# A recurrent cell computed by halves of its columns, with the last slot sums added straight out of PSUM

## The reference

```python
x = x + 0.5 * ffn(layernorm(x))
x = x + attn(layernorm(x))
x = x + 0.5 * ffn(layernorm(x))
```

```python
alpha = top-8 softmax of gelu(x @ w1.T + b1) @ w2.T      # T x 64
gi = (alpha.T @ x) / (alpha.sum(0) + 1e-8)               # 64 x 512 per sequence
gx = gi @ gru_wih.T + gru_bih ; gh = hs @ gru_whh.T + gru_bhh
r = sigmoid(xr + hr) ; z = sigmoid(xz + hz) ; n = tanh(xn + r * hn)
h_new = (1 - z) * n + z * hs
out = alpha @ (h_new @ wv.T + bv) @ wo.T + bo
```

## Time and profile before

| what | value |
|---|---|
| median of three runs | 3039.88 us (3039.07 to 3040.82) |
| the profiled execution | 3037.27 us, span 3035.4 us |
| PE busy | 2731.7 us (90%) |
| DVE busy | 1970.5 us (65%) |
| ACT busy | 1035.0 us (34%) |
| POOL busy | 1330.8 us (44%) |
| granted TensorE clock, mean | 0.964 of full speed |
| chain that ended last | PE 58%, DVE 29%, issue 8%, DMA 3% |

### The profile page before, as it was taken

How to read it: one execution, slowest core, us unless ns; L and a number is a source line. 1 busy time by engine, 2 the same in 40 slices (tenths; PEclk the granted TensorE clock), 3 DMA queues, 4 the chain that set the end, 5 groups by cost and what they waited for, 6 DMA issues and landing times.

```text
span 3035.4 us, 116733 instructions
## 1 busy us (share of the span) xinstructions
PE 2731.7 (90%) x51036; PEld 1942.8 (64%) x51036; DVE 1970.5 (65%) x5236; ACT 1035.0 (34%) x1891; POOL 1330.8 (44%) x1768
## 2 busy tenths in 40 slices
PE   7999789899899999999998999999999999989867
PEld 6787456666666666666666666666666666666643
DVE  6776456666666666666666666666766676666625
ACT  5776222333333333333233233333333332323220
POOL 2221444545444445444454445445555444445410
PEclk9999889999999999999999999999999999999978
DMA  7351112212122222212222222212122222212177
GB/s 228 96 162 52 41 47 67 56 32 59 53 60 60 60 60 60 58 55 52 60 60 56 56 60 60 56 44 51 53 60 60 60 60 59 63 46 56 42 257 290
DMA packets 365962, 224.75 MB, mean 74 GB/s; under 512 B 277584, under 2 KB 294032, under 8 KB 365456
## 3 DMA queue, kind: packets, MB, share of 16 engines
q1 hardware_dynamic: 356240, 200.51, 24.1%
q10 hardware_dynamic: 9216, 16.78, 1.5%
HBM read 125.49 MB, written 74.97 MB: 66 GB/s over the span
## 4 chain that ended last, share of the span: by engine, by line
PE 58%; DVE 29%; issue 8%; DMA 3%; POOL 1%; ACT 1%; SPq 1%; DVEq 0%; POOLq 0%; ACTq 0%
PE psum L875 14%; DVE blk L3133 10%; DVE blk L3131 10%; PE psum L1028 5%; PE psum L970 4%; PE psum L1050 4%; PE psum L1069 4%; PE psum L994 4%; PE psum L1037 4%; PE psum L779 2%; PE psum L951 2%; PE psum L1007 2%; PE psum L1090 2%; PE psum L930 2%; PE psum L716 1%
## 5 line engine op out<-in xcount | busy, mean ns | idle before, releaser
L875 PE MATMUL psum<-w_all,xnT 128*128 128x512 f32 (+2 forms) x2048 | 746.8, 501 | 21.3 <-DVE xc L3032 17.4
L2473 POOL TENSOR_TENSOR sm<-sm,half 128x1 f32<-128x1 f32 (+1 forms) x384 | 535.0, 1393 | 122.6 <-ACT sm L2048 106.6
L875 PEld LDWEIGHTS psum<-w_all,xnT 128*128 128x128 f32 x2048 | 363.9, 191 | 190.3 <-issue 145.0
L3131 DVE TENSOR_TENSOR blk<-blk 128x30 f32<-128x30 f32 (+14 forms) x960 | 398.8, 415 | 77.5 <-issue 50.7
L3133 DVE TENSOR_TENSOR blk<-blk 128x30 f32<-128x30 f32 (+14 forms) x960 | 427.2, 445 | 33.1
L930 PEld LDWEIGHTS psum<-xnT,w_all 128*128 128x128 f32 x2048 | 270.5, 202 | 75.6 <-issue 71.5
L930 PE MATMUL psum<-xnT,w_all 128*128 128x128 f32 x2048 | 295.6, 291 | 4.0 <-issue 4.0
L1050 PE MATMUL psum<-qg,st 32*32 32x64 f32 x8192 | 189.4, 228 | 87.8 <-DVE st L3149 53.8
L1069 PE MATMUL psum<-w_out,gate 128*128 128x512 f32 x512 | 253.0, 613 | 4.6 <-issue 2.5
L1050 PEld LDWEIGHTS psum<-qg,st 32*32 32x32 f32 x8192 | 140.6, 111 | 175.6 <-DVE st L3149 90.4
L3149 DVE STREAM_TRANSPOSE st<-psum 128x128 f32<-128x128 f32 x256 | 81.0, 316 | 201.2 <-PE psum L1050 198.2
(11 more groups left out here) (276 smaller groups left out, 4645.8 us busy)
## 6 DMA issues: line engine op xcount, KB each, us to landing
blk<-n_scratch SPq DMA_DIRECT2D x64, 512.0 KB, 4.4
xin<-in_L_attn_x_dram SPq DMA_DIRECT2D x96, 256.0 KB, 4.8
xh<-xc SPq DMA_DIRECT2D x64, 256.0 KB, 2.3
n_scratch<-nn SPq DMA_DIRECT2D x64, 256.0 KB, 3.4
e_scratch<-blk SPq DMA_DIRECT2D x32, 512.0 KB, 2.6
E<-e_scratch SPq DMA_DIRECT2D x64, 256.0 KB, 3.9
x_scratch<-xh SPq DMA_DIRECT2D x62, 256.0 KB, 3.7
rxn<-in_L_attn_x_dram SPq DMA_DIRECT2D x32, 256.0 KB, 2.9
```

The lines of the kernel that those rows point to most:

```text
L875: last = mm(dst, xnT[b][:, k * P:(k + 1) * P], w_all[:, k * WK + at:k * WK + at + n], start=(k == 0), stop=(k == KC - 1))
L2473: return g.tensor_tensor(dst, a, half[:, 0:n], ALU.pow)
L3131: own(tt(o, Y[:, 0:rows, s_:s_ + 1].to_broadcast([P, rows, cols]), N[:, s_:s_ + 1, s_ + 1:CH].to_broadcast([P, rows, cols]), ALU.mult))
```

## The change

Both cells are computed by halves of 256 columns, `lo` and `hi`, wherever the next engine can start on a half. DVE divides by halves, reading the sums where they lie: out of PSUM in the first cell (the copies by `slot_sums` go), from `slotacc` in the second. PE turns a half with two products into a bank of its own (`turned`), and ACT copies each half. The z product becomes two products of 256 columns in two banks (`z_at`), and so do its addition, its sigmoid, the last product and addition, the second transposes and copies. The bias of n is added to r's part before the n product is awaited. The value product takes its first term after the first half of the new state is copied.

Besides, the clearing for the attention stage moves into the first cell, between the division and the first gate. PE's wait for `aT` moves behind the r product. The last tile's slot sums are no longer copied by ACT and added by POOL: DVE adds them out of PSUM. ACT gets two operations of one element (`ask`), a Gelu ahead of `last_normal(NT, 0)` and an Exp ahead of `last_exp(NT, 0)`. SP's wait ahead of the twelve late loads has the new count of the same event, the end of the z product.

```diff
-            o_pe, o_act, o_dve = 6 * m, 5 * m, 7 * m
+            o_pe, o_act, o_dve = 9 * m, 8 * m, 9 * m
...
+                def turn(h):
+                    for k in range(2):
+                        last = tr(turned[h][:, k * P:(k + 1) * P], ht[:, (2 * h + k) * P:(2 * h + k + 1) * P], ident[:, :])
+                    last.then_inc(mid_pe, 1)
+
+                def gate_product(dst, j, c, n):
+                    for k in range(KC):
+                        if j == 0 and k % 2 == 0:
+                            e.wait_ge(mid_act, o_act + 1 + k // 2)
+                        last = mm(dst, giT[:, k * P:(k + 1) * P], wihT_at(k, j)[:, c:c + n], start=(k == 0), stop=(k == KC - 1))
+                    last.then_inc(mid_pe, 1)
+
+                def value(k):
+                    return mm(Bk[1][:, :], hTT[:, k * P:(k + 1) * P], voT_at(k), start=(k == 0), stop=(k == KC - 1))
...
+                turn(0)
+                e.wait_ge(mid_dve, o_dve + 2)
+                turn(1)
                 if m == 1:
                     e.wait_ge(wih_in, RELOAD)
...
+                gate_product(A[0][:, :], 0, 0, D)
+                e.wait_ge(aT, NT * (m + 1))
+                gate_product(C[0][:, :], 2, 0, D)
+                gate_product(z_at[0], 1, 0, HC)
+                gate_product(z_at[1], 1, HC, HC)
                 e.wait_ge(mid_dve, o_dve + 7)
+                turn(0)
+                e.wait_ge(mid_act, o_act + 7)
+                value(0)
+                e.wait_ge(mid_dve, o_dve + 8)
+                turn(1)
+                value(1)
+                e.wait_ge(mid_act, o_act + 8)
+                value(2)
+                value(3).then_inc(mid_pe, 1)
...
             pe.wait_ge(S["sums"], NT)
-            pe.wait_ge(aT, 2 * NT)
...
             def slot_copy(n):
+                if n == NT:
+                    return
...
             def last_normal(n, b):
+                if n == NT and b == 0:
+                    act(ask[0:1, 0:1], eps[0:1, 0:1], ACT.Gelu).then_inc(asked, 1)
...
             def last_exp(n, b):
+                if n == NT and b == 0:
+                    act(ask[0:1, 0:1], eps[0:1, 0:1], ACT.Exp).then_inc(asked, 1)
...
+                for c in (lo, hi):
+                    ts(ht[:, c], rows[:, c], s(0, "rden"), None, ALU.mult).then_inc(mid_dve, 1)
+                if m == 0:
+                    own(v.memset(slotacc[:, 0:D], 0.0))
+                    for b in range(B):
+                        own(v.memset(st[b][:, :], 0.0))
+                    own(v.memset(sums[:, :], 0.0))
+                ve.wait_ge(mid_pe, o_pe + 3)
                 tt(gr[:, :], A[0][:, :], gh[:, 0:D], ALU.add).then_inc(mid_dve, 1)
...
+                own(tt(gr[:, :], gr[:, :], bih_n[:, :], ALU.add))
                 ve.wait_ge(mid_pe, o_pe + 4)
+                tt(gn[:, :], C[0][:, :], gr[:, :], ALU.add).then_inc(mid_dve, 1)
+                ve.wait_ge(mid_pe, o_pe + 5)
+                tt(gz[:, lo], z_at[0], gh[:, D:D + HC], ALU.add).then_inc(mid_dve, 1)
+                ve.wait_ge(mid_act, o_act + 4)
                 own(tt(gr[:, :], hs[:, :], gn[:, :], ALU.subtract))
                 ve.wait_ge(mid_pe, o_pe + 6)
+                tt(gz[:, hi], z_at[1], gh[:, D + HC:2 * D], ALU.add).then_inc(mid_dve, 1)
+                for h, c in enumerate((lo, hi)):
+                    ve.wait_ge(mid_act, o_act + 5 + h)
+                    own(tt(gz[:, c], gz[:, c], gr[:, c], ALU.mult))
+                    tt(ht[:, c], gn[:, c], gz[:, c], ALU.add).then_inc(mid_dve, 1)
...
-            ve.wait_ge(S["sla"], NT)
+            ve.wait_ge(S["sla"], NT - 1)
+            ve.wait_ge(S["slot_ps"], both(NT, 1))
+            tt(slotacc[:, 0:D], slotacc[:, 0:D], slot_at[:, :], ALU.add).then_inc(S["slc"], 1)
```

More of the change, by code:

```diff
@@ L81, in build @@
         eps = sb("eps", 1)
+        ask = sb("ask", 1)
         h_bias = sb("h_bias", 2)
@@ L204, in build @@
         at_x, out_st = [sem(f"at_x{g}") for g in range(4)], sem("out_st")
+        asked = sem("asked")
         mid_pe, mid_act, mid_dve = sem("mid_pe"), sem("mid_act"), sem("mid_dve")
@@ L333, in build @@
         NMID = 4
+        HC = D // 2
+        turned = [ST[1], C[1]]
+        z_at = [A[1][:, 0:HC], ST[0][:, 0:HC]]
         def mid(e, m):
-            o_pe, o_act, o_dve = 6 * m, 5 * m, 7 * m
+            o_pe, o_act, o_dve = 9 * m, 8 * m, 9 * m
             if e is nc.tensor:
                 mm, tr = nc.tensor.matmul, nc.tensor.transpose
-                e.wait_ge(mid_dve, o_dve + 1)
[L341 to L345, removed]
+                def turn(h):
[10 more added lines that the diff above has]
+                    return mm(Bk[1][:, :], hTT[:, k * P:(k + 1) * P], voT_at(k), start=(k == 0), stop=(k == KC - 1))
+                e.wait_ge(mid_dve, o_dve + 1)
+                turn(0)
+                e.wait_ge(mid_dve, o_dve + 2)
+                turn(1)
@@ L346, in mid @@
                 if m == 1:
                     e.wait_ge(wih_in, RELOAD)
[L348 to L361, removed]
-                e.wait_ge(mid_dve, o_dve + 7)
+                gate_product(A[0][:, :], 0, 0, D)
+                e.wait_ge(aT, NT * (m + 1))
+                gate_product(C[0][:, :], 2, 0, D)
@@ new lines, in mid @@
+                gate_product(z_at[0], 1, 0, HC)
+                gate_product(z_at[1], 1, HC, HC)
+                e.wait_ge(mid_dve, o_dve + 7)
+                turn(0)
[7 more added lines that the diff above has]
+                value(3).then_inc(mid_pe, 1)
+                e.wait_ge(mid_dve, o_dve + 9)
@@ L363, in mid @@
             elif e is nc.scalar:
                 act = nc.scalar.activation
-                e.wait_ge(mid_pe, o_pe + 1)
-                act(giT[:, :], Bk[0][:, :], ACT.Copy).then_inc(mid_act, 1)
-                e.wait_ge(mid_dve, o_dve + 2)
+                for h in range(2):
+                    e.wait_ge(mid_pe, o_pe + 1 + h)
+                    act(giT[:, h * HC:(h + 1) * HC], turned[h][:, 0:HC], ACT.Copy).then_inc(mid_act, 1)
+                e.wait_ge(mid_dve, o_dve + 3)
                 act(gr[:, :], gr[:, :], ACT.Sigmoid).then_inc(mid_act, 1)
-                e.wait_ge(mid_dve, o_dve + 3)
+                e.wait_ge(mid_dve, o_dve + 4)
@@ L370, in mid @@
                 act(gn[:, :], gn[:, :], ACT.Tanh).then_inc(mid_act, 1)
[L371 to L374, removed]
+                for h in range(2):
+                    e.wait_ge(mid_dve, o_dve + 5 + h)
+                    act(gz[:, h * HC:(h + 1) * HC], gz[:, h * HC:(h + 1) * HC], ACT.Sigmoid).then_inc(mid_act, 1)
@@ L376, in _ @@
+                for h in range(2):
+                    e.wait_ge(mid_pe, o_pe + 7 + h)
+                    act(hTT[:, h * HC:(h + 1) * HC], turned[h][:, 0:HC], ACT.Copy).then_inc(mid_act, 1)
         @block.sync
@@ L704, in _ @@
                 x2_load(i)
-            sp.wait_ge(mid_pe, 6 + 4)
+            sp.wait_ge(mid_pe, 9 + 6)
             for i in range(N_DRAIN, min(N_MID, NT - 1)):
@@ L2983, in _, with mid_dve_part @@
             ve.wait_ge(ldw, 16 * 6)
[L2985 to L2993, removed]
-                own(v.reciprocal(s(0, "rden"), s(0, "den")))
-                own(ts(ht[:, :], slotacc[:, 0:D], s(0, "rden"), None, ALU.mult))
-                ve.nop().then_inc(mid_dve, 1)
-                ve.wait_ge(mid_pe, o_pe + 2)
+            def mid_dve_part(m, rows, total):
+                o_pe, o_act = 9 * m, 8 * m
+                lo, hi = slice(0, HC), slice(HC, D)
+                own(ts(s(0, "den"), total, 1e-8, None, ALU.add))
+                own(v.reciprocal(s(0, "rden"), s(0, "den")))
+                for c in (lo, hi):
[6 more added lines that the diff above has]
+                ve.wait_ge(mid_pe, o_pe + 3)
@@ L2998, in mid_dve_part @@
                 tt(gr[:, :], A[0][:, :], gh[:, 0:D], ALU.add).then_inc(mid_dve, 1)
[L2999 to L3001 removed]
+                ve.wait_ge(mid_act, o_act + 3)
                 own(tt(gr[:, :], gr[:, :], gh[:, 2 * D:3 * D], ALU.mult))
[L3003 removed]
+                own(tt(gr[:, :], gr[:, :], bih_n[:, :], ALU.add))
@@ L3013, in mid_dve_part @@
+                ve.wait_ge(mid_pe, o_pe + 9)
                 stt(sv[:, :], Bk[1][:, :], 0.5, bvo[:, :], ALU.mult, ALU.add).then_inc(mid_dve, 1)
             ve.wait_ge(sl_ps, both(NT, 1))
-            slot_sums(0, A[0][:, :], Bk[1][:, 0:1])
-            mid_dve_part(0)
-            own(v.memset(slotacc[:, 0:D], 0.0))
+            ve.wait_ge(last_sums, 1)
+            mid_dve_part(0, A[0], Bk[1][:, 0:1])
             def since(sem_, value):
@@ L3678, in _ @@
             last_dve()
-            ve.wait_ge(S["sla"], NT)
+            ve.wait_ge(S["sla"], NT - 1)
+            ve.wait_ge(S["slot_ps"], both(NT, 1))
+            tt(slotacc[:, 0:D], slotacc[:, 0:D], slot_at[:, :], ALU.add).then_inc(S["slc"], 1)
+            ve.wait_ge(S["slc"], NT)
             ve.wait_ge(last_sums, 2)
-            own(v.tensor_copy(slotacc[:, D:D + 1], lg_at[0][:, 0:1]))
-            mid_dve_part(1)
```

(1 more changed line is left out.)

8 lines of the change are left out of this document (removed).

## The result

The changed kernel took 3011.36 us in the median (2995.32 to 3015.71, four runs), the kernel before 3039.57 us beside it (3039.07 to 3040.82, four runs): a ratio of 0.9897, 95% interval [0.9859, 0.9935]. The forecast was 3026.1 us with a range of 3018 to 3034.

The account below looks back on a forecast made before the run. TensorE, busy nine tenths of the span, and the serial chain of waits through both cells were taken to bound the kernel. Terms of 7.3 (first cell) and 6.5 (second) made 13.8: 3039.88 - 13.8 = 3026.1 us, range 3018 to 3034.

Parts of the forecast that it names:

- its first: Opening step on what bounds the kernel: the change touches two short serial cells and nothing of the attention stage between.
- the two `ask`: Early Gelu and Exp operations on ACT around the last tile: no gain, cost taken as 0, bound 0.2 us.
- Rival 2: Attention stage, shifted 7 us, falls into other clock steps: gain lost, chance 0.08, or a like gain, 0.07.
- Head of the first cell: First read of the totals to first gate product: product starts near 292.15 instead of 293.80, 1.65 us gained.
- Products of the first cell: Three gate products there: same work, less time at half clock, 1.8 us gained, bounds nothing and 2.5.
- the value product: Eight instructions at each cell's end: clock may stay up or fall late, 1.2 us gained in both cells.
- From z to the value product: Stretch of 4.79 us after the z product, shortened by halves: 1.8 to 2.2 us gained, taken as 2.0.
- Clearing: Clearing ahead of the attention stage, mostly hidden in DVE's wait for the r product: 0.6 us gained, not 1.9.
- Second cell: Cell after the attention stage: head 3.3, gate products 0, z to value product 2.0, value product 1.2; together 6.5 us.
- rival 4: Head of the second cell: the moved wait brings nothing, as something else holds ACT's copies; 3029.5 us, chance 0.05.
- rival 3: Final pass: transfers bind it, capping the second cell's gain near 7; 3025 to 3027 us, chance 0.05.
- the count seems stable: Attention stage: the count of long clock steps was taken as stable because three runs lay within 1.8 us.

Follow-up runs that it names:

- before_wait2: Kernel before with two more clearings of slotacc between first cell and attention stage: median 3042.57 us, ratio 0.9998.
- after_wait19: Changed kernel with nineteen more clearings of slotacc between first cell and attention stage: median 3017.39 us, ratio 0.9919 to the kernel before.
- after_last: Changed kernel with the tile `ask` allocated last, so that no other tile moves: median 3031.04 us, ratio 0.9965 to the kernel before.
- after_last_2: Second set of runs of after_last, on another chip: median 3028.44 us, ratio 0.9962 to the kernel before.
- after_again: The changed kernel itself, unaltered, run once more: median 3012.98 us, ratio 0.9905 to the kernel before.
- first_only: Kernel before with only the first cell by halves and the moved clearing, second cell and last slot sums old: median 3028.30 us, ratio 0.9952.
- own_buffer: Changed kernel with the last transposed weights copied to `slt`, so ACT need not wait for the previous tile's store: median 3016.09 us, ratio 0.9902 to the kernel before.
- move64: Kernel before with an unused `ask` tile of 16 elements, moving all later tiles by 64 bytes: median 3047.91 us, ratio 1.0000.

## Why the prediction was wrong, step by step

**The step that failed** is its first: that the change touches "nothing of the long attention stage between them", and with it the costing of the two `ask` at 0 by their operations alone. The operations showed no cost. Their tile moved nearly all the others by 32 bytes, E among them, and that was worth -12.4 +- 4.3 and -11.7 +- 5.2 us in the kernel before and 18.3 +- 7.1 in the changed one, where E with the tiles behind it gives 11.1 +- 5.6. Why the place matters so much stays open. Rival 2 had the right stage, with a chance of 0.07, and the wrong mechanism; no run shows an effect of the start of the stage against the clock (before_wait2, after_wait19, after_last).

Without the moved tiles the change is worth 11.3 and 11.6 us (after_last, after_last_2), near the 13.8 forecast. With them it is 28.2 in the medians of the result and 29.6 in after_again. If the tiles are taken at the 12 us that they gave the kernel before, 11.5 and 12 make 23.5; the rest lies inside the intervals and was not explained. Nor is every kernel in line with the sum: first_only gained 6 us more than its cell, and after_wait19 some 7 more than 15.7 + 12 - 10.4.

**Head of the first cell**, forecast 1.65: from the first read to the product 3.70 us before and 1.85 after, 1.85 gained.

**Products of the first cell**, forecast 1.8: 2.28 gained, near the bound of 2.5 that stood for a clock that never falls. That is what happened: the granted clock was 1.00 in every stretch read between 288 and 309 us, for instance

```profile
300.00:301.00 1.00, 1.00 (x6) 0.73 (x4) 0.55 (x1) 0.40 (x1) 0.00 (x0) 1.00 0.00 0
```

where the earlier trace rows had 0.71 at 298 to 299, on the way up from 0.50. The same holds for **the value product** of that cell: 1.80 gained, forecast 1.2. These two are clock terms of the sum, both too small. The eight profiled kernels with the new first cell all took 10.60 us for the products and 20.65 or 20.64 for the cell; with the old one the products took 12.04 to 13.63 us in twelve traces and the cell 27.7 to 30.4 (before_wait2, with its two clearings, left out). So the trace of before gives 9.2 where others would give 7.0 to 9.8.

**From z to the value product**, forecast 2.0: 2.61 gained, since the working took the second pair of transposes off here, while its 0.22 us lay in the value product. **Clearing**, forecast 0.6: 0.64. Together 9.2 for 7.3.

**Second cell**, forecast 6.5 and measured 6.5. That they agree so closely is partly luck: from ACT's copy to `sv` the old form took 26.0 to 28.6 us in twelve traces, and the new one 19.2 to 21.9 in seven. In this pair the head gained 3.37 for 3.3, the products 0.13 for 0, the rest 2.98 for 3.2. Here the clock did fall and came back inside the value product:

```profile
2942.00:2943.00 1.00, 1.00 (x3) 0.48 (x2) 0.00 (x0) 0.38 (x1) 0.00 (x0) 0.50 0.81 303
2943.00:2944.00 1.00, 1.00 (x3) 0.39 (x3) 0.00 (x0) 0.00 (x0) 0.00 (x0) 0.87 0.97 332
```

The wait moved to ACT, as said, and the head gained what rival 4 doubted; own_buffer shows 1.55 us still in it.

**The two `ask`**, forecast 0:

```profile
2896.09 1.28 ACT L2109 ACT_TABLE_LOAD   x1
2897.38 0.20 ACT L2109 ACTIVATE ask<-eps 1x1 f32<-1x1 f32 x1
2897.49 0.80 ACT L2112 ACTIVATE rxn<-xh,sm 128x512 f32<-128x512 f32 x1
```

The normalisation ended at 2898.29, and TensorE took it at 2900.01, so 1.7 us of cover were left. The next operation began 0.01 us after the load. The Trainium skill (ScalarE: Activation LUTs, What ACT_TABLE_LOAD costs) adds a drain of about 1380 ns to each switch of table; these rows show none, as the earlier trace rows did not, and the measurement decides. **Transfers** (rival 3) did not bind: the final pass, from `sv` on, took 47.9 us for 49.1, although 303 and 332 GB/s already flow beside the value product of the second cell, in the rows above.

**The spread.** The prediction read "the count seems stable" from three runs within 1.8 us. Over 22 to 29 runs on one chip the kernel before spreads 13 to 25 us, so the bound of 0.2% between faster and no change needed more runs than were shown.

## What to carry to other kernels

A new tile is part of a change even if nothing uses it: compare the addresses in the two compiled programs, and cost the transfers into every tile whose place within 128 bytes moves. Measure a one-tile shift of the kernel before as a control ahead of crediting an edit, and look at the median landing of each load in both traces. Where a serial chain is cut into halves, cost the products after it at both levels of the clock. Here the first cell's products stayed at 1.00 with 1.1 us of idle TensorE ahead and began at 0.50 with 2.7 us in the trace of before; whether that carries over to another kernel was not tried. Compare several traces of each kernel before a term of a few microseconds is called measured.

## What the runs showed of the hardware

Loads of 256 KB in pieces of 128 bytes landed in a median 3.2 to 3.7 us where the tile began at a multiple of 128 bytes (13 profiled kernels), and in 4.0 to 4.3 us where it began 32 bytes below or above one (7 kernels), both from 350 to 2650 us of each trace. Whether 64 would do for E was not tried. The Trainium skill (DMA: Bandwidth & Descriptors, How a descriptor splits into AXI transactions) says, by the vendor's account, that a transaction which reads has to start at a multiple of 256 bytes. An estimate by that rule and the addresses: half of E's pieces straddle such a boundary at the old place and at move64's, and none at the new one. The landings of E agree, if the rule also holds for a write into SBUF; they do not show that it is the cause. The store out of nn reads SBUF in pieces of 128 bytes too, and there the place hardly shows: a median of 3.3 to 3.4 us where nn began at a multiple of 128 bytes (7 kernels), 3.4 to 3.5 elsewhere (13).
